# Half of a unit's values are biased on TensorE and expanded on ScalarE instead of VectorE

## The reference

```python
q = (layernorm(x) @ Wq + bq).reshape(N, L, 16, 8)
k = (ctx @ Wk + bk).reshape(N, L, 16, 8)
v = (ctx @ Wv + bv).reshape(N, L, 16, 8)
qp, kp = elu(q) + 1, elu(k) + 1
# per head, over time t: sums += outer(kp[t], v[t]); res[t] = qp[t] @ sums
out = (res / cumsum(qp, axis=1)).reshape(N, L, 128) @ Wo + bo
x = x + out
x = x + moe(layernorm(x))     # top 2 of 8 experts, silu(g) * u, down
```

## Time and profile before

| | |
|---|---|
| median of 3 runs | 403.84 us (401.23 to 405.92) |
| the profiled execution | 400.13 us, its span 398.4 us |
| mean granted TensorE clock | 0.901 |
| busy over the span | TensorE 313.8 us (79%), VectorE 277.0 us (70%), ScalarE 231.0 us (58%), GpSimd 219.3 us (55%) |
| attention, units 0 to 7 | from about 14 us to about 192 us of the span |

### The profile page before, as it was taken

How to read it: one execution, slowest core, us unless ns; L and a number is a source line. 1 busy time by engine, 2 the same in 40 slices (tenths; PEclk the granted TensorE clock), 3 DMA queues, 4 the chain that set the end, 5 groups by cost and what they waited for, 6 DMA issues and landing times.

```text
span 398.4 us, 12299 instructions
## 1 busy us (share of the span) xinstructions
PE 313.8 (79%) x4430; PEld 255.4 (64%) x4430; DVE 277.0 (70%) x770; ACT 231.0 (58%) x464; POOL 219.3 (55%) x301
## 2 busy tenths in 40 slices
PE   6797989869797977767878886779899999988400
PEld 5575756547574755557657775568788888877400
DVE  5799998797988989894745754467556556635355
ACT  4786867584775859604656834346566566646300
POOL 6202065785858688784785586545545555654300
PEclk9899988998889899865989998699999999999955
DMA  7221404114050310111322222353575574221099
GB/s 267 92 95 43 133 2 157 32 20 157 14 169 22 112 38 16 35 35 42 61 63 61 48 61 69 113 83 112 170 204 151 149 214 141 48 56 36 6 302 330
DMA packets 47722, 39.45 MB, mean 99 GB/s; under 512 B 32550, under 2 KB 39084, under 8 KB 47664
## 3 DMA queue, kind: packets, MB, share of 16 engines
q1 hardware_dynamic: 43344, 30.20, 26.5%
q0 software_dynamic: 4320, 8.47, 7.0%
HBM read 15.16 MB, written 12.21 MB: 69 GB/s over the span
## 4 chain that ended last, share of the span: by engine, by line
PE 40%; DVE 26%; ACT 11%; issue 8%; another core or an unknown queue 7%; DMA 5%; SPq 2%; DVEq 0%; ACTq 0%; POOLq 0%
PE scores L1204 6%; DVE Pm L884 5%; PE bank L1366 4%; PE bank L1364 4%; PE bank L1365 3%; PE bank L1345 3%; PE bank L1347 3%; ACT hid_hi L777 3%; DVE Kexp L1117 2%; PE bank L1346 2%; DVE Vexp L856 2%; DMA w_hi<-by_token 2%; PE scores L1347 2%; PE scores L1345 2%
## 5 line engine op out<-in xcount | busy, mean ns | idle before, releaser
L601 POOL DMA_INDIRECT by_token<-y_sb,row_meta x71 | 79.8, 1124 | 73.1 <-ACT y_sb L761 58.2
L528 POOL DMA_INDIRECT by_expert<-token_rows,rows_to x64 | 69.2, 1081 | 31.5 <-issue 17.7
L1117 DVE TENSOR_TENSOR Kexp<-hid,hid_hi 128x512 f16<-128x512 f32 x71 | 49.1, 693 | 50.4 <-ACT hid_hi L777 47.9
L1111 DVE SCALAR_TENSOR_TENSOR hid<-scores,silu 128x512 f32<-128x512 f32 x71 | 47.4, 686 | 24.2 <-remote 8.0
L1204 PE MATMUL scores<-qT,Kexp 32*128 32x128 f32 (+1 forms) x1024 | 44.0, 315 | 16.3 <-DVE Pm L884 13.7
L1204 PEld LDWEIGHTS scores<-qT,Kexp 32*128 32x128 f32 x1024 | 39.1, 221 | 26.0 <-DVE Pm L884 20.8
L777 ACT ACTIVATE hid_hi<-hid 128x512 f16<-128x512 f32 x71 | 44.6, 628 | 19.0 <-DVE hid L1111 10.5
L1364 PE MATMUL bank<-w_hi,hid_hi 128*128 x248 | 45.3, 223 | 9.3 <-DVE Kexp L1117 7.3
L770 ACT ACTIVATE silu<-bank 128x512 f32<-128x512 f32 x71 | 40.5, 597 | 20.1 <-remote 8.7
L1365 PE MATMUL bank<-w_lo,hid_hi 128*128 x248 | 44.5, 222 | 2.5 <-issue 2.4
L884 DVE TENSOR_TENSOR Pm<-scores,causal 128x512 f32<-128x512 f32 x64 | 41.1, 684 | 6.4 <-ACT Pm L683 5.3
(11 more groups left out here) (291 smaller groups left out, 741.2 us busy)
## 6 DMA issues: line engine op xcount, KB each, us to landing
w_raw<-in_w_pack_dram SPq DMA_DIRECT2D x8, 768.0 KB, 4.6
x_all<-in_x_tok_dram SPq DMA_DIRECT2D x8, 256.0 KB, 5.1
cT<-in_ctx_t_dram SPq DMA_DIRECT2D x8, 256.0 KB, 4.5
w_hi<-by_token SPq DMA_DIRECT2D x4, 512.0 KB, 7.4
w_lo<-by_token SPq DMA_DIRECT2D x4, 512.0 KB, 8.0
out_dram<-x_all SPq DMA_DIRECT2D x8, 256.0 KB, 6.3
by_expert<-pad_row SPq DMA_DIRECT2D x9, 130.0 KB
by_token<-y_sb,row_meta POOLq DMA_INDIRECT x71
```

Of the source, the lines that this page charges most:

```text
L528: pool.indirect_dma_start(by_expert, bass.IndirectOffsetOnAxis(ap=rows_to[u % 2][:, s, b:b + 1], axis=0), token_rows[u % 2][:, b, s, :], N ...
L601: pool.indirect_dma_start(by_token, bass.IndirectOffsetOnAxis(ap=row_number[:, i % METAS, s, 1:2], axis=0), y_sb[:, k, s, :], None, bounds ...
L1117: dve.tensor_tensor(hid_lo[:, k % 2, slot, :], hid[:, slot, :], hid_hi[:, k % 2, slot, :], ALU.subtract).then_inc(lo_done, 1)
```

## The change

The bias of the first half of a unit's values is now put into the PSUM bank by one more product on TensorE, a row of ones with `bv_b` repeated for four chunks (contraction 1, 512 columns), and the 8 value products accumulate onto it. ScalarE then copies the half into `Vexp` in two instructions (`front_v0`), which VectorE no longer does. VectorE keeps the second half with its bias (`front_v1`). The semaphore `vexp_done` becomes `vexp0_done` and `vexp1_done`, and each waiter takes the one of its half. `front_v0(u + 1)` stands in ScalarE's body right after `off_scores(u, 0)`, ahead of the weight casts `weights`; in the body of unit 0 it stands behind the weight casts and ahead of `front_neg(1, 0)`. For unit 0 it stands before the loop.

```diff
+            def front_v0(u, par):
+
+                act.wait_ge(v_ps, 2 * u + 1)
+                if first(u):
+                    act.wait_ge(cleared, 1)
+                elif u == 1:
+                    act.wait_ge(cleared, 2)
+                else:
+                    act.wait_ge(av_done, UB * (u - 1))
+                for a in range(2):
+                    rows = slice(a * CH, a * CH + CH)
+                    src = value_bank(u, 0)[rows, :].rearrange("p (c g a k) -> p c g a k", g=RJ, a=2, k=HD)[:, :, :, a, :]
+                    act.activation(Vexp[par][rows, 0:NCH // 2, :, a * HD:(a + 1) * HD], src, ACT.Copy).then_inc(vexp0_done, 1)
...
             def body(u, par):
                 off_scores(u, 0)
+                if not first(u) and not last(u):
+                    front_v0(u + 1, 1 - par)
                 for m in range(3):
                     weights(u, par, m)
+                if first(u):
+                    front_v0(1, 1)
                 if not last(u):
                     front_neg(u + 1, 0)
                     front_exp(u + 1, 0)
...
             front_keys(0, 0, range(1))
+            front_v0(0, 0)
             units(act, body)
...
-            def front_v(u, par):
-                for half in range(2):
-                    dve.wait_ge(v_ps, 2 * u + half + 1)
-                    for a in range(2):
...
+            def front_v1(u, par):
+                dve.wait_ge(v_ps, 2 * u + 2)
+                for a in range(2):
...
-                    pe.wait_ge(vexp_done, 4 * u + 2)
+                    pe.wait_ge(vexp0_done, 2 * u + 2)
                 pe.matmul(bank[1], Wk_s, cT[par][:], start=True, stop=True).then_inc(k_ps, 1)
...
+                if half == 0:
+                    pe.matmul(value_bank(u, 0).rearrange("p (c d) -> p c d", d=D), ones[0:1, :], bv_b[0:1, :].unsqueeze(1).to_broadcast([1, NCH // 2, D]),
+                              start=True, stop=False, skip_group_check=True)
                 for c in range(half * NCH // 2, (half + 1) * NCH // 2):
                     ps = value_bank(u, half)[:, (c % 4) * P:(c % 4 + 1) * P]
                     for a in range(2):
-                        ins = pe.matmul(ps[a * CH:(a + 1) * CH, :], cT[par][:, c, :], Wv_s, start=True, stop=True)
+                        ins = pe.matmul(ps[a * CH:(a + 1) * CH, :], cT[par][:, c, :], Wv_s, start=(half == 1), stop=True, skip_group_check=(half == 0))
```

More of the change, by code:

```diff
@@ L242, in attention_moe_kernel @@
         kexp_done = sem("kexp_done")
-        vexp_done = sem("vexp_done")
+        cleared = sem("cleared")
+        vexp0_done = sem("vexp0_done")
+        vexp1_done = sem("vexp1_done")
         z_done = sem("z_done")
@@ L845, in elu_q @@
                 dve.scalar_tensor_tensor(qT[par][:], bank[0][:], bq_one[:], expn[:, 1, :], ALU.add, ALU.max).then_inc(qk_done, 1)
-            def front_v(u, par):
-                for half in range(2):
-                    dve.wait_ge(v_ps, 2 * u + half + 1)
-                    for a in range(2):
-                        rows = slice(a * CH, a * CH + CH)
-                        cs = slice(half * NCH // 2, (half + 1) * NCH // 2)
-                        src = value_bank(u, half)[rows, :].rearrange("p (c g a k) -> p c g a k", g=RJ, a=2, k=HD)[:, :, :, a, :]
-                        dst = Vexp[par][rows, cs, :, a * HD:(a + 1) * HD]
-                        bvv = bv_b[rows, :].rearrange("p (g a k) -> p g a k", g=RJ, a=2)[:, :, a, :]
-                        dve.tensor_tensor(dst, src, bvv.unsqueeze(1).to_broadcast([CH, NCH // 2, RJ, HD]), ALU.add).then_inc(vexp_done, 1)
+            def front_v1(u, par):
+                dve.wait_ge(v_ps, 2 * u + 2)
+                for a in range(2):
+                    rows = slice(a * CH, a * CH + CH)
+                    src = value_bank(u, 1)[rows, :].rearrange("p (c g a k) -> p c g a k", g=RJ, a=2, k=HD)[:, :, :, a, :]
+                    dst = Vexp[par][rows, NCH // 2:NCH, :, a * HD:(a + 1) * HD]
+                    bvv = bv_b[rows, :].rearrange("p (g a k) -> p g a k", g=RJ, a=2)[:, :, a, :]
+                    dve.tensor_tensor(dst, src, bvv.unsqueeze(1).to_broadcast([CH, NCH // 2, RJ, HD]), ALU.add).then_inc(vexp1_done, 1)
             def front_z(u, par):
@@ L1047, in body @@
                 if not last(u):
-                    front_v(u + 1, 1 - par)
+                    front_v1(u + 1, 1 - par)
                 if not first(u):
@@ L1080, in first_keys @@
                                       ALU.mult).then_inc(kexp_done, 1)
-            dve.memset(Vexp[0][:], 0.0)
+            dve.memset(Vexp[0][:], 0.0).then_inc(cleared, 1)
             front_stats(0, 0)
@@ L1090, in _ @@
             dve.tensor_reduce(headmask[:], headsel[:].rearrange("p r j -> p j r"), AX_X, ALU.add).then_inc(const_dve, 1)
-            dve.memset(Vexp[1][:], 0.0)
+            dve.memset(Vexp[1][:], 0.0).then_inc(cleared, 1)
             dve.wait_ge(const_dve, 5)
@@ L1099, in _ @@
             dve.wait_ge(const_loaded, 16)
-            front_v(0, 0)
+            front_v1(0, 0)
             dve.wait_ge(const_made, N_MADE)
@@ L1162, in front_transpose_x @@
                 if not first(u):
-                    pe.wait_ge(vexp_done, 4 * u + 4)
+                    pe.wait_ge(vexp1_done, 2 * u + 2)
                 for b in range(UB):
@@ L1181, in front_values @@
                 if u == 1 and half == 0:
-                    pe.wait_ge(vexp_done, 2)
+                    pe.wait_ge(vexp0_done, 2)
                 elif not first(u):
                     pe.wait_ge(qk_done, 2 * u - 1 + half)
+                if half == 0:
+                    pe.matmul(value_bank(u, 0).rearrange("p (c d) -> p c d", d=D), ones[0:1, :], bv_b[0:1, :].unsqueeze(1).to_broadcast([1, NCH // 2, D]),
+                              start=True, stop=False, skip_group_check=True)
                 for c in range(half * NCH // 2, (half + 1) * NCH // 2):
@@ L1210, in values @@
                 if b == 0:
-                    pe.wait_ge(vexp_done, 4 * (u + 1))
+                    pe.wait_ge(vexp0_done, 2 * (u + 1))
+                    pe.wait_ge(vexp1_done, 2 * (u + 1))
                     if not first(u):
```

## The result

| | before | after |
|---|---|---|
| median of 4 runs | 402.53 us (400.96 to 405.92) | 416.75 us (415.04 to 421.71) |
| the profiled execution | 400.13 us, span 398.4 us | 416.94 us, span 415.2 us |
| mean granted TensorE clock | 0.901 | 0.877 |

The change makes the kernel slower: the ratio is 1.0397, 95% interval 1.0341 to 1.0452. That is +14.2 us between the medians where +4.5 was forecast, and 416.75 lies above the range (404.0 to 412.5).

The account below looks back on a forecast made before the run. VectorE at each body's head and TensorE before the scores of b = 3 were taken to bound the attention: +3.6 (body 0) + 0.8 (1) + 0.8 (2 to 4) + 0.1 (5) - 0.8 (6) = +4.5, 408.3 us, range 404.0 to 412.5.

Parts of the forecast that it names:

- part 2: Before the scores of b = 3, the added product costs TensorE 1.07 us, +0.27 net in a body like 3.
- The sum at a full clock: All bodies' terms added: +4.5 us, giving 404.6 on the profiled execution and 408.3 on the median.
- body 1: Product 1.07 less slack 0.18 before the last mask and 0.1 gained at the head: +0.8 us.
- bodies 3 to 5: Gain 0.8 at the head, pay 1.07: +0.27 in bodies 3 and 4; body 5 has slack, +0.1.
- body 6: Projects no values, so it has the gain at the head and no price: -0.8 us.
- The head's gain: At the start of a body, the first mask and VectorE's work behind it can start 0.87 us earlier.
- Part 1: Head of a body: ScalarE's copy pair takes 0.9 us, keys wait less; gain 0.8 in bodies 2 to 6.
- Part 3: Body 0 and start: ScalarE's new wait makes `off_scores(0, 1)` 2.8 us later, the product adds 0.8: +3.6.
- Rival 3: Clock falls more often: 1.75 us in body 0, 2.1 for two products at the lower clock, 412.2; chance 0.20.
- Rival 2: Fuller TensorE keeps its clock in bodies 2 to 5, giving back at most 7.3 us, 401.0; chance 0.12.
- Rival 1: The product fits beside other work in bodies 1 to 5, so only heads count: -1.3, 402.5 us; chance 0.10.

Follow-up runs that it names:

- e1_seed_full: The changed kernel with its added bias product at contraction 128 instead of 1: ratio 1.0179 to the kernel before.
- g2_seed_full: The changed kernel with its added bias product at contraction 128, the same kernel as e1_seed_full, run in the last group: ratio 1.0180.
- e8_all_full: The changed kernel with all three kinds of bias products at contraction 128: ratio 1.0206.
- The square: Added product at contraction 1 or 128, on one chip: copy on ScalarE (changed kernel) 1.0269 and 1.0180, copy on VectorE (kernel before) 1.0475 and 1.0252.
- e5_before_again: The kernel before, unchanged, one run on the chip of the second group: 364.18 us.
- e2_no_seed: The changed kernel without the added bias product, so the first half of the values lacks its bias: ratio 1.0029.
- g1_after: The changed kernel, unchanged, run again in the last group: ratio 1.0269.
- e6_after_again: The changed kernel, unchanged, run again in the second group: ratio 1.0274.
- e3_seed_only: The kernel before with only the one-row bias product added, VectorE still expanding all parts with the bias: ratio 1.0419.
- e7_tail_full: The kernel before with its own two one-row bias products made at contraction 128: ratio 0.9956.
- e12_seed_f16: The changed kernel with the added bias product made of two float16 products at contraction 128: ratio 1.0167.

## Why the prediction was wrong

The sign was right, slower, and the size forecast a third of what came.

- **The step that failed** is in part 2: "since the stretch is a bounded time, the extra product mostly pushes other work out of its end, at the full clock; I keep 1.07". It took the clock around the product as given. With the clock as in before, the change costs 1.8 to 2.1% (`e1_seed_full`, `g2_seed_full`, `e8_all_full`; by the medians of all runs 1.0 to 2.3%), that is about 7 us of 400; with the one-row product it costs 2.7 to 4.0% (by the medians 3.3 to 3.8%). The square shows that this second part comes with the contraction, and the profiles of the result have 42.7 us at the half clock against 25.0. By what mechanism one row goes with a lower clock stays open.
- **The sum at a full clock.** Forecast were 4.5 us (1.1%), the ratios give some 7. In the pair of profiles on one chip, `e8_all_full` against `e5_before_again`, the spans differ by 8.8 us, and half of that, 4.4, is there at the last `tail_o` (184.68 against 180.25), as much as the sum said. The other 4.4 lie in the experts' part, 186.6 against 182.2, where the kernels don't differ and for which I had taken nothing: a shift at the end of the attention did not move the end by as much. Why is open; in the two profiles of the result that part differs by 1.5 us.
- **That the 4.4 fits is partly luck**, for the terms don't. Body 0 grew by 2.8 (forecast 3.6), body 1 by 0.1 (0.8), body 2 shrank by 0.2 and the bodies 3 to 5 grew by 0.6 each (0.27, 0.27, 0.27 and 0.1), body 6 grew by 0.8 (forecast -0.8), body 7 shrank by 0.7 (0). The head's gain is real (the first mask comes 2.69 instead of 3.60 us after `tail_o`), and bodies of `e2_no_seed` at the full clock are shorter by it. With the product in, the bodies 3 to 5 of `e8_all_full` are bound by the loop over GpSimd, which the gain doesn't enter. I read ScalarE as the only one that waits for the scores of b = 3; that GpSimd waited for them too, 13.9 us in all, stood in the trace of before, though not in its chain.
- **Part 1, the copy.** Taken 0.9 us for the pair, measured 0.76 to 0.78; no wait of the key projection in the body of unit 3: right.
- **Part 3, body 0.** Forecast +3.6, of which 2.8 up to `off_scores(0, 1)`. That came only 0.85 later, since the values there took 1.97 us instead of 3.16: the half clock, which I had carried over from before, lay elsewhere this time. It began at 23.3, and there it cost more: body 0 grew by 6.9 us. `g1_after` shows the same 39.2 us, `e6_after_again` 34.2 with no half clock at all, so the long stretch comes and goes with the run or the chip.
- **Rival 3** was nearest, more time at the lower clock, and priced it by the stretches of before: 3.5 us at half speed. The stretch was 13.7 us long. Its second half, two products at double price, missed that it is the work around the products that pays: of the eight added products in the profile one ran wholly and one partly at the half clock. `e3_seed_only` shows a ratio of 1.04 without ScalarE's wait, so the pause isn't a condition of the loss.
- **Rival 2**, the fuller TensorE keeps its clock, is refuted for this product: 17.1 us more of TensorE's busy time and a clock of 0.877 instead of 0.901. The rule behind it, that activity lifts the throttle (the Trainium skill, "TensorE: Matmul & The Clock Gate", section "The HAM clock gate"), doesn't fit the stretch 24 to 37 above, busy for 13.00 of 13 us at a clock of 0.50. The ends of matmul records are modelled, so this busy time may hold gaps.
- **Rival 1**, the product fits beside other work, is refuted by `e2_no_seed` against `e1_seed_full` on one chip: 1.0029 and 1.0179, intervals apart.

**What stays open:** why a one-row product goes with a lower clock, and by which rule its place decides where the clock falls; why before's own one-row products show no such effect in `e7_tail_full`; why before itself keeps its clock on one chip and loses 25 us to it on another; why the experts' part, the same code, takes 182 to 187 us in the profiles of the first two groups; whether the place of the product counts; and the 33.1 us of `e12_seed_f16`.

## What to carry to other kernels

Before TensorE is given a small extra product, ask what it does to the granted clock of the work around it, and try it with the full contraction if the data allow it: here that didn't lengthen the product and took the loss from 4.8 to 2.5% (copy on VectorE) and from 2.7 to 1.8% (copy on ScalarE), though before's own two products gained nothing sure by it. A gain at one place of a body counts only if the loop that bounds the body goes through it; follow every engine that waits for the instruction ahead of which the price is put, and read the chain on each chip, since here it differed. When the clock is part of the time, compare on one chip and with several runs of each, since the place of its falls changes from run to run.

## What the runs showed of the hardware

- An f32 product of 512 columns takes two records. At the full clock it took 1.12 us from start to end with one row of contraction (first product in body 0 of `g1_after`), and 1.02 and 1.12 with 128 rows (first and second in body 0 of `e1_seed_full`); at the half clock 2.07 (`g1_after`, at 29.77). The contraction hardly shows in the product's own time, but in the clock: 27.2 to 42.7 us at the half one in the profiles with the added one-row product, 5.2 to 17.7 with 128 rows in its place.
- A busy TensorE didn't by itself bring the clock back: in the profile after it stayed at 0.50 for 13 us of uninterrupted records. And the same wait of 1.15 us went with a fall of the clock in one run of the kernel and with none in another.
- A ScalarE copy of 64 x 256 out of PSUM takes 0.36 to 0.38 us, two in a row 0.76 to 0.78 (the profile after).
- The same kernel took 364.2 us on one chip and 400.1 us on another; 23.7 of the 36 us lie in the experts' part (205.9 us against 182.2), where the granted clock was 0.93 and 0.92.
